# Cross attention of a decoder layer: scores as three rounded products, queries turned first, the output projection moved ahead of the first scores

## Chip, cores, metric

One Trainium2 chip, one of its cores. The metric is the device time of the whole program in microseconds (us), the median of three runs. The program holds two decoder layers; the change touches one stage of the first.

## Reference, cut to the stage

Batch 16, 112 query rows of 512 features, 375 context rows. Sixteen heads of 128, in eight groups of keys and values. The stage computes the second half of the layer's attention (`xout`), and adds its part of the projection to x:

```python
def _gqa(q, k, v):
    scale = 1.0 / np.sqrt(q.shape[-1])
    scores = jnp.einsum('bsghd,btgd->bghst', q, k) * scale
    p = jax.nn.softmax(scores, axis=-1)
    return jnp.einsum('bghst,btgd->bsghd', p, v)

qx = _fp8_linear_pertensor(ln_out, wqx, wqx_scale, qx_in_scale).reshape(b, s, g, hpg, d)
qx = _ln(qx, qxln_w, qxln_b)
kvx = jnp.einsum('bsi,oi->bso', cond, w_kv_x)
kx, vx = jnp.split(kvx, 2, axis=-1)
kx = _ln(kx.reshape(b, sc, g, d), kxln_w, kxln_b)
vx = vx.reshape(b, sc, g, d)
xout = _gqa(qx, kx, vx).reshape(b, s, nh * d)
cat = jnp.concatenate([core, xout], axis=-1)
catq = _div_clamp_fp8(cat, proj_smooth)
return jnp.einsum('bsi,oi->bso', catq, wproj) * (proj_in_scale * proj_w_scale)
```

## The kernel before

`normed_attention` (L613) is used twice, for self attention (`own` true) and for cross attention (`own` false); the change is to the second use. Its loop has 32 steps: the 16 sequences with the first eight heads, then the 16 sequences with the other eight. A step b has these parts:

- Eight `unit`s (L862), each a product of 512 columns in one PSUM bank: 0 and 1 are queries (four heads each), 2 to 4 are keys of 125 context rows each, 5 to 7 (from `LU` = 5) are values. Context and weights are held as a rounded high part and a low part (type f32r), so that a unit of keys or values is 12 matmuls (`product`, L31: high x high, low x high, high x low), a unit of queries 8.
- VectorE measures and normalises queries and keys (`measure`, `aggregate`, `normalise`, L1159 to L1181), with a root by GpSimd (L818).
- `turn` (L901): TensorE transposes eight heads of queries, then four tiles of keys (375 columns each). ScalarE evicts each with the affine part of the normalisation (`take_turned`, L1068) into `qT` and `kT`, f32.
- `scores` (L936), eight of them (heads 0 to 7), each an f32 matmul of 375 columns; VectorE takes the maxima (`top`, L1183), ScalarE the exponentials (L1081), VectorE divides (L1189 to L1201), TensorE transposes (`turn_probs`, L951), ScalarE evicts (`take_probsT`, L1091), TensorE weighs values in pairs of heads (`weigh_values`, L965).
- VectorE scales the result and prepares its rounding (L1203 to L1220), GpSimd rounds it (`round_cat`, L834), TensorE projects (`project_out`, L922: 16 matmuls of 512 columns), VectorE adds to x (`add_out`, L1244). This rounding and projection of step b - 1 lie in step b.

Query rows are padded from 112 to 128 with rows of another sequence, so that in every eighth step (b % 8 = 7, `spread`) the queries are already there, in `spread_room`, and units 0 and 1 are left out. GpSimd copies these rows (`keep_spread`, L827).

The order is written out by hand for each engine, and each engine works its queue in that order. TensorE in step b (L1008 to L1025): unit 5; last values of step b - 1; unit 6; `turn`; unit 7; scores 0 and 1; `project_out(b - 1)`; then for t from 0 to 7: scores t + 2, one of the units 0 to 4 of step b + 1 (after t = 0, 2, 3, 4, 5), `turn_probs` t, and values of a pair for t = 3, 5, 7. ScalarE (L1103): cast of the next queries' input; values 0, 1; `take_turned`; values 2; exponentials 0 and 1; `split_ctx(b + 1)` (L1060); then for each t exponential t + 2 and `take_probsT` t. VectorE (L1260, L1313): maxima 0 and 1; division 0 and 1; `split_ctx(b + 1)` (low part, L1156); `add_out(b - 1)`; from step 18 on `measure_row` (L1251); then for t = 0 the maxima of head 2, the measuring of unit 0, and so on.

`turn_probs` t waits for `probsT_ready` of the transposition before it, since all but the last share PSUM bank 5 (L957). Scores use banks 2, 3, 4 in turn (L748), turned tiles banks 6, 7, 5, 3, 2, 4 (`TBANK`, L644), the weighed values banks 6 and 7, the projection bank 6, the units banks 0 and 1.

## Time and profile before

| | |
|---|---|
| median of 3 runs | 3532.51 us (3528.98 to 3533.45) |
| profiled execution | 3518.53 us, its span 3516.8 us |
| granted TensorE clock, mean | 0.969 of full |
| cross attention | from about 855 to 2095 us of the span |
| busy over the span | TensorE 92%, VectorE 68%, ScalarE 49%, GpSimd 23% |
| one step of the cross attention (902.43 to 941.14) | 38.71 us |

How to read the rows below. PE is TensorE, DVE VectorE, ACT ScalarE, POOL GpSimd. A timeline row has start and duration in us, engine, line of the kernel, operation, what it writes and reads, its shape, how many like it in a row (x4), and in brackets how long the engine had been idle before it and for whom. A matmul's duration is its streaming and some 0.17 to 0.18 us until its end is known; the pace of several is seen in their starts. An f32 matmul makes two records (x2 for one). A row of the stretch table has the stretch, its length, then busy time (count) of PE, PEld (weight load), DVE, ACT and POOL, then the granted clock of TensorE (1.00 full, 0.50 half), the DMA share and GB/s. Matmuls through `product` all stand under L42.

### The profile page before, as it was taken

Reading aid. Unit: us, or ns where it says so; the run is one execution under the profiler, and the core shown is the slowest. Engines: PE = TensorE matmul, PEld = TensorE weight load, DVE = VectorE, ACT = ScalarE, POOL = GpSimd, SP = SyncE. Lnnn points to the kernel's source line nnn. Section 1 sums busy time; section 2 is a strip of 40 time slices with the busy share of each in tenths; the row PEclk is TensorE's granted clock in tenths of the full one; section 3 lists DMA queues with packets and bytes.
Section 4 is the critical chain, followed back from the end, with each engine's and each line's share of the span. In section 5 each row is a group of like instructions: output and inputs, shape, how many; then the busy total and the mean of one; then the engine's idle time right before and its main releaser. Section 6 shows DMA issues by size and latency. Waiting matters only on the chain. (4 is left out here: it accounts for less than half of the span.)

```text
span 3516.8 us, 50927 instructions
## 1 busy us (share of the span) xinstructions
PE 3249.5 (92%) x17776; PEld 2635.9 (75%) x17776; DVE 2386.7 (68%) x6147; ACT 1724.9 (49%) x4169; POOL 793.6 (23%) x936
## 2 busy tenths in 40 slices
PE   5858998997999999999999989999989979998999
PEld 4647877885787888778777867888868757776788
DVE  5997878786666666767667757899765555557433
ACT  5984455444344334443344333788537755452222
POOL 0004444452222222332222224000223310000000
PEclk9879999999999999999999999999999989999999
DMA  6121010002000000210000016999820124543000
GB/s 234 29 61 32 1 49 25 1 27 77 21 21 30 21 23 20 85 38 22 21 21 30 20 42 223 362 404 398 318 60 2 49 107 137 152 138 120 13 12 19
DMA packets 121167, 304.67 MB, mean 87 GB/s; under 512 B 42336, under 2 KB 45920, under 8 KB 115152
## 3 DMA queue, kind: packets, MB, share of 16 engines
q1 hardware_dynamic: 114752, 283.74, 23.0%
q0 software_dynamic: 6160, 17.67, 1.7%
q8 instruction: 144, 2.36, 0.3%
q14 instruction: 111, 0.91, 0.1%
HBM read 255.32 MB, written 45.35 MB: 85 GB/s over the span
## 5 line engine op out<-in xcount | busy, mean ns | idle before, releaser
L42 PE MATMUL bank<-w,cross_ctx_part 128*125 128x512 f32 x1536 | 519.8, 420 | 2.8 <-DVE cross_kn L1179 2.8
L42 PEld LDWEIGHTS bank<-w,cross_ctx_part 128*125 128x125 f32 x1536 | 283.4, 187 | 83.9 <-DVE cross_kn L1179 8.5
L1087 ACT ACTIVATE cross_prob<-bank,cross_neg_max 112x375 f32<-112x375 f32 x256 | 147.0, 574 | 347.5 <-DVE cross_neg_max L1185 347.5
L42 PE MATMUL bank<-w_low,cross_ctx_part 128*125 128x512 f32 x768 | 303.2, 395 | 0.0
L1185 DVE TENSOR_REDUCE cross_neg_max<-bank 112x1 f32<-112x375 f32 x256 | 134.2, 525 | 208.8 <-PE bank L947 205.7
L42 PE MATMUL bank<-moe_wt,moe_zT 128*128 128x448 f32 x1176 | 262.1, 371 | 0.6 <-DVE moe_wt L1872 0.6
L1872 DVE TENSOR_TENSOR moe_wt<-moe_raw,moe_wt 128x1792 fp32r<-128x1792 f32 (+1 forms) x111 | 231.6, 2108 | 14.5 <-ACT moe_wt L1767 13.5
L42 PE MATMUL bank<-mlp_zT,mlp_signs 128*128 128x512 f32 (+1 forms) x1024 | 221.0, 369 | 6.2 <-DVE mlp_zT L2620 6.2
L42 PEld LDWEIGHTS bank<-moe_wt,moe_zT 128*128 128x128 f32 x1176 | 213.5, 188 | 15.5 <-DVE moe_wt L1872 0.8
L42 PE MATMUL bank<-w,self_xq 128*128 128x512 f32 (+1 forms) x464 | 196.8, 424 | 22.6 <-DVE w_low L601 21.3
L1767 ACT ACTIVATE moe_wt<-moe_raw 128x1792 fp32r<-128x1792 f32 (+1 forms) x111 | 196.8, 1775 | 28.5 <-DMA moe_raw<-in_moe_w 16.8
L42 PEld LDWEIGHTS bank<-mlp_zT,mlp_signs 128*128 128x128 f32 x1024 | 177.7, 189 | 43.4 <-issue 6.4
L821 POOL TENSOR_TENSOR cross_ve<-cross_mv,eps 125x4 f32<-125x4 f32 (+1 forms) x152 | 30.3, 199 | 720.7 <-DVE cross_mv L1170 720.7
L42 PE MATMUL bank<-w_low,self_xq 128*128 128x512 f32 (+1 forms) x464 | 188.2, 406 | 0.0
L1100 ACT ACTIVATE cross_probT<-bank 125x336 f32<-125x336 f32 x256 | 111.3, 447 | 154.8 <-PE bank L961 154.7
L1179 DVE TENSOR_SCALAR cross_kn<-bank,cross_mv,cross_rstd 125x128 f32<-125x128 f32 x384 | 131.1, 404 | 80.4 <-POOL cross_rstd L824 80.2
L1066 ACT ACTIVATE cross_v<-bank 125x512 f32<-125x512 f32 x96 | 57.4, 598 | 237.8 <-PE bank L975 130.6
L947 PE MATMUL bank<-cross_kT,cross_qT 128*112 128x375 f32 x448 | 173.3, 478 | 0.0
L961 PEld LDWEIGHTS bank<-ident,cross_prob 112*125 112x125 f32 x768 | 116.5, 189 | 72.9 <-issue 40.0
L42 PEld LDWEIGHTS bank<-w_low,cross_ctx_part 128*125 128x125 f32 x768 | 143.4, 187 | 36.2
L975 PE MATMUL bank<-cross_probT,cross_v 125*128 125x224 f32 x768 | 169.9, 358 | 0.0
L42 PE MATMUL bank<-moe_wt,moe_hT 128*128 128x512 f32 x588 | 148.3, 402 | 12.2 <-issue 12.2
(436 smaller groups left out, 8131.4 us busy)
## 6 DMA issues: line engine op xcount, KB each, us to landing
moe_raw<-in_moe_w SPq DMA_DIRECT2D x74, 896.0 KB, 7.4
moe_raw<-in_moe_w SPq DMA_DIRECT2D x37, 1024.0 KB, 8.3
stream<-in_L1f SPq DMA_DIRECT2D x32, 768.0 KB, 7.7
cross_ctx_raw<-in_ctxT SPq DMA_DIRECT2D x32, 750.0 KB, 4.3
wide_ctxT<-in_ctxT SPq DMA_DIRECT2D x16, 750.0 KB, 4.2
wide_ctx_rows<-in_ctx SPq DMA_DIRECT2D x16, 750.0 KB
expert_rows<-a_zeros SPq DMA_DIRECT2D x1, 8960.0 KB, 25.7
moe_zrow<-expert_rows SPq DMA_DIRECT2D x35, 256.0 KB, 7.8
```

What stands on the lines that cost most here:

```text
L42: mm = pe.matmul(out, a, b, start=first and n == 0, stop=last and n == len(pairs) - 1)
L821: pool.tensor_tensor(ve[0:rows, n, :], mv[0:rows, n, :, 1], k.eps[0:rows, 0:4], ALU.add)\
L947: mm = pe.matmul(score_bank(t)[0:S, i * NK:(i + 1) * NK], queries[:, h, 0:S], keys[:, h // 2, 0:NK], start=True, stop=True)
L961: mm = pe.transpose(probs_bank(t)[0:KN, at:at + S], prob[:, t % SLOTS, i, j * KN:(j + 1) * KN], k.ident[0:S, 0:S])
L975: mm = pe.matmul(ps[6 + pair // 2][:, at:at + 2 * S], v[:, j, pair * P:(pair + 1) * P], probsT_of(pair, j), start=j == 0, stop=j == KT - 1)
L1066: act.activation(v[:, j, :], unit_bank(b, LU + j)[0:KN, :], ACT.Copy).then_inc(s["v_ready"], 1)
L1087: op = act.activation(prob[:, t % SLOTS, i, :], score_bank(t)[0:S, i * NK:(i + 1) * NK], ACT.Exp, bias=neg_max[:, h:h + 1], accum_out=tota ...
L1100: act.activation(probT[:, (t // 2) % 2, :, t % 2, :], probs_bank(t)[0:KN, 0:KT * S].rearrange("p (j t) -> p j t", t=S), ACT.Copy).then_inc ...
L1179: op = dve.tensor_scalar(out, unit_bank(b, n)[0:rows, h * P:(h + 1) * P], mv[0:rows, n, h, 0:1], rstd[0:rows, n, h:h + 1], ALU.subtract, A ...
L1185: dve.tensor_reduce(neg_max[:, HS * t:HS * (t + 1)], score_bank(t)[0:S, 0:HS * NK].rearrange("p (h n) -> p h n", h=HS), AX.X, ALU.max, neg ...
L1767: act.activation(wt[:, PLACES[n % 4], 0, 0:w], raw[:, n % RAW, 0:w], ACT.Copy).then_inc(s["w_high"], 1)
L1872: dve.tensor_tensor(wt[:, PLACES[n % 4], 1, 0:w], raw[:, n % RAW, 0:w], wt[:, PLACES[n % 4], 0, 0:w].bitcast(F32), ALU.subtract).then_inc( ...
```

## The change

- Scores of the cross attention become three f32r products of 376 columns (`product` of `qT_high`, `qT_low`, `kT_high`, `kT_low`); the 376th column is a zero pad, set once. ScalarE evicts each turned tile twice, raw and rounded (`split_turned`). GpSimd subtracts to make the low parts (`queries_low`, `keys_low`; in a spread step `spread_queries_low`), which lie where the raw ones lay.
- `turn` is split: the queries are turned first in a step, ahead of unit 5, the keys where they were. In step 0 the queries wait for the last normalisation. ScalarE evicts the queries first in its step, ahead of the cast. Turned tiles use banks 2, 3, 5, 6, 4, 7.
- `project_out(b - 1)` goes ahead of scores 0 and 1 where there is a next step with query units (`out_first`); it also waits for the eviction of key tile 1. Where there is none, it stays behind them.
- GpSimd's `round_cat(g - 1)` stands in step g behind the low parts of the queries and ahead of those of the keys; before it stood at the end of step g - 1's queue.
- The bf16 tiles `clipped` and `magic` now lie in `probT`.

```diff
-    TBANK = [2, 3, 4] if own else [6, 7, 5, 3, 2, 4]
+    TBANK = [2, 3, 4] if own else [2, 3, 5, 6, 4, 7]
...
+            qT_high, kT_high = sb("qT", [P, H, P], F32R), sb("kT", [P, GR, NK + 1], F32R)
+            qT, qT_low = raw_and_low(k, ctx, "cross_qT", [P, H, P])
+            kT, kT_low = raw_and_low(k, ctx, "cross_kT", [P, GR, NK + 1])
...
+            def turned_by(g, n):
+                pool.wait_ge(s["turned_raw"], turned_no(g, n))
+                pool.wait_ge(s["turned_ready"], turned_no(g, n))
+
+            def queries_low(g, n):
+                turned_by(g, n)
+                heads = slice(4 * n, 4 * n + 4)
+                pool.tensor_copy(spread_qT[:, heads, spread_rows(g)], qT[:, heads, S:]).then_inc(s["spread_ready"], 1)
+                pool.wait_ge(s["spread_ready"], 2 * tiles(g) + n + 1)
+                pool.tensor_tensor(qT_low[:, heads, :], qT[:, heads, :], qT_high[:, heads, :].bitcast(F32), ALU.subtract)\
+                    .then_inc(s["turned_low"], 1)
...
+            def keys_low(g, n):
+                turned_by(g, n)
+                pool.tensor_tensor(kT_low[:, n - 2, 0:NK], kT[:, n - 2, 0:NK], kT_high[:, n - 2, 0:NK].bitcast(F32), ALU.subtract)\
+                    .then_inc(s["turned_low"], 1)
...
-                if not spread(g):
+                if own and not spread(g):
                     keep_spread(g)
+                if not own:
+                    if spread(g):
+                        spread_queries_low(g)
+                    for n in range(0 if spread(g) else 2):
+                        queries_low(g, n)
+                    if g:
+                        round_cat(g - 1)
+                    for n in range(2, TG):
+                        keys_low(g, n)
...
-            def turn(b):
-
-                if not own:
-                    wait(pe, s["cat_scaled"], 2 * b)
+            def turn_queries(b):
                 for g in range(0 if spread(b) else 2):
-                    pe.wait_ge(s["normed"], norm_no(b, g))
+                    pe.wait_ge(s["normed"], norm_no(b, LU - 1 if not own and b == 0 else g))
...
+            def turn_keys(b):
+
+                if not own:
+                    wait(pe, s["cat_scaled"], 2 * b)
...
+                if not own and not at_end:
+                    pe.wait_ge(s["turned_raw"], turned_no(b + 1, 3))
+                    pe.wait_ge(s["turned_ready"], turned_no(b + 1, 3))
...
+                    if t == 0 and spread(b):
+                        pe.wait_ge(s["spread_low"], b // GROUP + 1)
+                    if t in (0, 2, 6):
+                        pe.wait_ge(s["turned_low"], turned_no(b, (2, 4, 4, 5)[t // 2]))
+                    if t >= 3:
+                        pe.wait_ge(s["exp_done"], NS * b + t - 2)
+                    mm = product(pe, score_bank(t)[0:S, 0:NK + 1], [q[:, t, 0:S] for q in (qT_high, qT_low)],
+                                 [key[:, t // 2, :] for key in (kT_high, kT_low)], True, True)
...
+                    turn_queries(b)
                     unit(b, LU)
                     if not first:
                         weigh_values(b - 1, GR - 1)
                     unit(b, LU + 1)
-                    turn(b)
+                    turn_keys(b)
                     unit(b, LU + 2)
+                    out_first = not first and one_more and has(b + 1, 0)
+                    if out_first:
+                        project_out(b - 1)
                     scores(b, 0)
                     scores(b, 1)
-                    if not first:
+                    if not first and not out_first:
                         project_out(b - 1)
...
+            def split_turned(b, n):
+                act.wait_ge(s["turned_in_psum"], turned_no(b, n))
+                for first, to in ((qT, kT), (qT_high, kT_high)):
+                    out = to if n >= 2 else first
...
+                    op = act.activation(out, ps[TBANK[n]][:, 0:out.shape[1]], ACT.Identity, scale=head_ln[:, at:at + 1],
+                                        bias=head_ln[:, at + 1:at + 2])
...
+                if not own:
+                    split_queries(b)
                 if one_more:
                     cast(b + 1)
...
                     take_values(b, 0)
                     take_values(b, 1)
-                take_turned(b)
+                    for n in range(2, TG):
+                        split_turned(b, n)
                 take_values(b, KT - 1)
```

## Rows read from the trace of the kernel before

**Rows 1.** The page, busy time and share of the span.

```profile
PE 3249.5 (92%) x17776; PEld 2635.9 (75%) x17776; DVE 2386.7 (68%) x6147; ACT 1724.9 (49%) x4169; POOL 793.6 (23%) x936
```

**Rows 2.** The table of stretches, one step of the cross attention (step 1 to 2).

```profile
902.43:941.14 38.71, 38.71 (x190) 31.11 (x188) 25.77 (x96) 15.77 (x35) 10.06 (x13) 1.00 0.08 24
```

**Rows 3.** The timeline of step 12, TensorE.

```profile
1313.33 0.78 PE L42 MATMUL bank<-w,cross_ctx_part 128*125 128x512 f32 x2
...
1316.26 1.30 PE L975 MATMUL bank<-cross_probT,cross_v 125*128 125x224 f32 x6
...
1320.18 1.03 PE L908 MATMUL bank<-ident,cross_qn 128*128 128x128 f32 x8
...
1325.12 1.42 PE L947 MATMUL bank<-cross_kT,cross_qT 128*112 128x375 f32 x4
...
1326.61 0.40 PE L42 MATMUL bank<-wo_low,cross_catq 128*112 128x512 f32 x1
...
1329.84 0.39 PE L42 MATMUL bank<-wo_low,cross_catq 128*112 128x512 f32 x1
...
1333.67 0.55 PE L961 MATMUL bank<-ident,cross_prob 112*125 112x112 f32 x3
```

**Rows 4.** The timeline of step 12, ScalarE, GpSimd and VectorE.

```profile
1320.88 1.45 ACT L1078 ACTIVATE cross_qT<-bank,head_ln 128x512 f32<-128x512 f32 x2
...
1321.79 1.90 POOL L838 TENSOR_TENSOR cross_catq<-cross_scaled,cross_magic 128x896 fp32r<-128x896 f32 x1
1322.22 2.32 ACT L1078 ACTIVATE cross_kT<-bank,head_ln 128x375 f32<-128x375 f32 x4
...
1327.73 1.45 ACT L1060 ACTIVATE cross_ctx_part<-cross_ctx_raw 128x1500 fp32r<-128x1500 f32 x1
...
1329.21 1.72 DVE L1156 TENSOR_TENSOR cross_ctx_part<-cross_ctx_raw,cross_ctx_part 128x1500 fp32r<-128x1500 f32 x1 [0.73 <-ACT cross_ctx_part L1060]
...
1331.45 0.54 DVE L1185 TENSOR_REDUCE cross_neg_max<-bank 112x1 f32<-112x375 f32 x1
...
1333.07 0.45 ACT L1100 ACTIVATE cross_probT<-bank 125x336 f32<-125x336 f32 x1 [0.39 <-PE bank L961]
```

**Rows 5.** Timelines elsewhere: f32r products of 256 and of 448 columns.

```profile
3466.83 3.13 PE L42 MATMUL bank<-mlp_zT,mlp_signs 128*128 128x256 f32 x25
...
2149.64 0.97 PE L42 MATMUL bank<-moe_wt,moe_zT 128*128 128x448 f32 x4
```

**Rows 6.** GpSimd's low parts by line; the timeline of step 19.

```profile
L594 POOL TENSOR_TENSOR w_low<-w_raw,w x8: 1272/1308/2277, 1439.5 to 1465.8; 128x512 fp32r<-128x512 f32 x8
...
1617.06 0.69 DVE L1254 BATCH_NORM_STATS2 cross_row_stats<-x 112x6 f32<-112x512 f32 x1
...
1619.38 0.55 PE L961 MATMUL bank<-ident,cross_prob 112*125 112x112 f32 x3
```

**Rows 7.** The timeline of step 0, which has no output projection.

```profile
840.74 2.83 DVE L1179 TENSOR_SCALAR cross_kn<-bank,cross_mv,cross_rstd 125x128 f32<-125x128 f32 x8
...
854.37 2.06 PE L947 MATMUL bank<-cross_kT,cross_qT 128*112 128x375 f32 x6
...
860.09 0.54 DVE L1185 TENSOR_REDUCE cross_neg_max<-bank 112x1 f32<-112x375 f32 x1
...
861.81 0.55 PE L961 MATMUL bank<-ident,cross_prob 112*125 112x112 f32 x3 [2.59 <-ACT cross_probT L1100]
```

**Rows 8.** TensorE's idle times (timeline), and the clock behind them (table of stretches).

```profile
842.21 0.71 PE L42 MATMUL bank<-w,cross_ctx_part 128*125 128x512 f32 x2 [2.79 <-DVE cross_kn L1179]
...
1450.64 0.55 PE L961 MATMUL bank<-ident,cross_prob 112*125 112x112 f32 x3 [3.70 <-ACT cross_probT L1100]
...
843.60:847.00 3.40, 3.40 (x10) 2.61 (x9) 0.00 (x0) 0.45 (x1) 0.00 (x0) 0.50 0.00 0
861.80:865.20 3.40, 3.39 (x17) 2.77 (x18) 2.84 (x11) 1.01 (x3) 1.21 (x2) 1.00 0.48 194
...
1451.20:1454.60 3.40, 3.40 (x8) 2.34 (x8) 2.74 (x9) 1.54 (x5) 0.89 (x1) 0.50 0.94 355
```

61 lines of the change are left out of this document (42 added, 19 removed).

## Prediction

> **What bounds the kernel now.** I read the page's busy shares first: TensorE is busy 92% of the span [rows 1]. Then the stretch table of one step of the cross attention, because only that stage (855 to 2095 us, 32 steps) is changed: in a step of 38.71 us TensorE is busy for all of it, VectorE 25.8, ScalarE 15.8, GpSimd 10.1 [rows 2]. So the stage looks bound by TensorE's work, and cheaper scores look like pure gain. The timelines show why that is not enough. In step 12 [rows 3] TensorE starts the last value units at 1313.33, the first scores at 1325.12 (11.79 later; I call the start of scores 0 S), and transposes the second head's probabilities at 1333.67, S + 8.55. Beside it [rows 4], the other engines are busy with one strict chain from S on, since ScalarE and VectorE work their queues in written order: maxima and exponentials of heads 0 and 1, ScalarE's high part of the next context (1327.73, 1.45), VectorE's low part (1329.21, 1.72), the addition of the output rows, the maxima of head 2 (1331.45, S + 6.33), its exponential, and only then `take_probsT` of head 0 (1333.07), for which the second transposition waits. During these 8.55 us TensorE does four scores, the output projection, query unit 0 and one transposition. The chain and TensorE's work end nearly together there: ScalarE had idled only 0.39 us for TensorE. The output projection is what covers the chain.
>
> **Cost of a score.** The projection's second product starts at 1326.61, its sixteenth at 1329.84 [rows 3]: 3.23/14 = 0.231 for each f32r product of 512 columns, 3.70 for the sixteen. The first of them would so start at 1326.38, and the two scores ahead, from 1325.12, take 1.26, 0.63 each. The new ones are three f32r products of 376 columns. The trace has f32r products of 256 and 448 columns [rows 5]: 25 in 3.13 us, less 0.28 for a single one, is 0.119 each; 4 in 0.97, less 0.37, is 0.200. Between them on a line 376 columns give 0.17, so a score 0.51 and a gain of 0.12. Bounds of one product: 0.119 and 0.231 (512 columns), a score 0.36 to 0.69. If all 256 gains counted: 31 us. The Trainium skill (FP8 and Floating Point Precision, TensorE Precision Notes) says true f32 goes through the array in four passes; the trace agrees (0.63 us for 375 columns), and three passes for four would by that rule alone be 0.47 a score, and the sum below 4 us less.
>
> **Queries turned first, and its cost at the top of a step.** The same eight transpositions (1320.18, 1.03 less 0.17 until the end is known: 0.87 us) [rows 3], only earlier; nothing for TensorE. ScalarE now evicts each turned tile twice, raw and rounded: two more of 128x512 and four more of 128x375. Back to back they take 1.45/2 = 0.73 and 2.32/4 = 0.58 [rows 4], so 3.8 us more of ScalarE a step, out of 23 idle. Whether that blocks anything I follow from the top T of step (1313.33 before). TensorE: turned queries to T + 0.87, value unit to 3.7, last values of the step before to 4.8, value unit to 7.6, keys turned to 8.9, value unit to 11.8; then the projection. ScalarE: queries from 0.6 to 3.6, cast, values at 5.0 and 7.8, then keys at 0.58 each: key tile 1 (the one that holds the projection's bank 6) is out at about 10.8, the last at 13.1. Cover 1.0 us. GpSimd: two query tiles (0.29 + 1.31 each, [rows 6] for 128x512) done at 5.5; then `round_cat`, which before ended at 1321.79 + 1.90 = 1323.69, that is 6.3 after the last values end (1316.26 + 1.13) [rows 3, 4], so now T + 11.2. TensorE asks for it at 11.8: cover 0.6. Then four key tiles; 128x375 costs between 0.8 (in proportion to 896 columns at 1.90) and 1.31, I take 1.1: done at 12.3, 13.4, 14.5, 15.6. Scores 0 come at T + 15.5 behind the projection, scores 2, which want three tiles, at 16.5. So all this is hidden; if the cover is gone it costs what runs over, 1:1. VectorE's queue is not changed.
>
> **The projection ahead of the scores.** `out_first` holds for steps 1 to 29 without 6, 14 and 22: 26 steps. S moves from T + 11.79 to 11.79 + 3.70 = T + 15.49. Everything in the chain above hangs on S or is queued behind something that does: the exponentials on scores 0 and 1, `split_ctx` of the next step behind them on ScalarE, its low part, `add_out` and the maxima of head 2 behind it on VectorE. So the chain moves 3.70 later with S, while the 3.70 of TensorE work that covered it now lies before it. Step 0 has no projection, and shows this directly [rows 7]: S = 854.37, the maxima of head 2 at S + 5.72, the second transposition at 861.81 = S + 7.44 after 2.59 us of idle TensorE. It has no `add_out` either; steps 1 to 17 have it, and their maxima of head 2 come 6.33 - 5.72 = 0.61 later. Less 0.12 for the faster first score, the second transposition comes at S + 7.44 + 0.61 - 0.12 = S + 7.93. TensorE gets there at four scores 2.04 + unit 1.85 + transposition 0.32 = S + 4.2. It stands still for 3.7 us. From step 18 on `measure_row` (0.69 us, [rows 6]) is also ahead of the maxima, some 0.6 more: S + 8.53, a stall of 4.3. Before, that row reading was hidden but for 0.1: in step 19 (S = 1610.74) the second transposition came at 1619.38, S + 8.64 [rows 6].
> Sum of a step, up to 17: S + 3.70, chain 7.93 - 8.55 = -0.62, four later scores at -0.12 = -0.48, together +2.60. From 18 on: 3.70 - 0.12 - 0.48 = +3.10. Behind the stall nothing catches up, since TensorE had no other idle time in the step. Steps 1 to 17 that count: 14 (15 apart), +36.4; 18 to 29: 11, +34.1. Step 15: its maxima wait for VectorE's weight splitting, there TensorE idled 3.70 already [rows 8], so the projection moves into time that was lost anyway: 0. Step 0: queries now turned ahead of the first value unit, behind VectorE's last key normalisation, which ends at 840.74 + 2.83 = 843.57 where TensorE resumed at 842.21 [rows 7, 8]: +1.4, less 0.1. Steps 6, 14, 22, 30 and 31 keep the scores first; scores 0 wait for GpSimd's first key tile (12.3 for 11.8, +0.6) and the later scores give 0.5 back; GpSimd's last key tiles run beside VectorE: +0.5 each, +2.5. Sum without the clock: 36.4 + 34.1 + 1.3 + 2.5 = **+74**.
>
> **The clock.** TensorE's granted clock fell from full (2.4 GHz) to half (1.2) after it had idled 2.79 us (842.21) and after 3.70 us (1450.64), and stayed at half for about 3.4 us of work each time; after the 2.59 us in step 0 it stayed full [rows 8]. A half-speed stretch of 3.4 us costs 1.7. The new stalls, 3.7 and 4.3 us, are as long as the longer of these or longer, in 25 steps, in each of which TensorE is the bound afterwards. Bounds: 0 (as after 2.59) and 3.4 (two such stretches running); I take 1.7, by the 3.70 row: 25 x 1.7 = **+43**. The Trainium skill (TensorE: Matmul & The Clock Gate, Part 1) has the rule that activity releases the throttle and idleness brings it back; the trace agrees, and without that rule the sum would be +74.
>
> Total 74 + 43 = +117. The profiled execution, 3518.5 us (span 3516.8), would become about 3636. It lies 14 us under the median of the timed runs, so I add the sum to the median: 3532.5 + 117 = **3650**.
>
> **The rivals.** (A) The stall comes, the clock doesn't fall or falls rarely: for it, the case of 2.59; against it, two falls at 2.79 and 3.70. 3532.5 + 74 = 3607. Chance 0.2. (B) The other side: TensorE stays the bound, because the next context's split and the maxima of head 2 get done early enough, as they would if they didn't hang on S; then 256 scores at -0.12 give -31: 3502. The point from which it decides: the second transposition must be ready by S + 4.2; step 0, without the projection, had it at 7.44. Chance 0.07. (C) GpSimd overruns: `round_cat` has 0.6 of cover at the projection; if the low parts take as long as 128x896 (1.90), the queries end at about 6.6 and let it start in time (11.2 less its two 1.9 is 7.4), but a key tile at 1.9 makes scores 2 wait for T + 16.9, 0.4 later: 25 x 0.45 = 11, 3661. Beside it: the Trainium skill (SBUF — State Buffer, SBUF: two separate sides) states that GpSimd and a VectorE operation with two SBUF inputs lock each other out of one port pair; by that rule a low part that meets `cat_clipped` would be held for its 0.6 us, the same size; the trace agrees that a low part can be held, 2.28 for a median of 1.31 [rows 6]. Chance 0.05. (D) The f32r products go at the pace of 512 columns: a score 0.69, the four later ones +0.24 for -0.48, 25 x 0.72 = 18: 3668. Chance 0.04. (E) The cut: if part of the stall is absorbed so that it just pays for the scores, no change. Nothing in the rows absorbs it. Chance 0.02.
>
> **How the numbers follow.** Forecast 3650, chance 0.62. A measurement of this kernel can tell about 0.2%, 7 us, from no change. Faster: B, 0.07. Same: E, 0.02. Slower: forecast, A, C and D, 0.91. The range goes from below A, 3595, to the forecast with two half-speed stretches in about half of the steps together with C or D, 3690 (1.7 x 13 + 18 = 40 more).
>
> **What would show it.** TensorE's wait for `take_probsT` at L961 should be about 100 us in all, once a step, some 3.6 long up to step 17 and 4.2 from 18; S-to-S about 41.3 to 43 for 38.71; scores 0.51 each; the maxima of head 2 at S + 6.2; no wait at `project_out`; half clock after most of the stalls. Wrong would be: maxima of head 2 much before S + 6, a wait ahead of the projection, a period of 37.7.

## The result, and the profile after

| | before | after |
|---|---|---|
| median | 3532.98 us (4 runs) | 3661.74 us (4 runs, 3657.19 to 3670.66) |
| ratio | 1 | 1.0367 (1.0354 to 1.038) |
| profiled execution, its span | 3518.53, 3516.8 | 3670.66, 3668.9 |
| granted TensorE clock, mean | 0.969 | 0.944 |

Slower by 129 us, 3.7%; the forecast was 3650, in 3595 to 3690. The page of after, busy time, answers to [rows 1]: TensorE's share falls although it has 256 more matmul records, GpSimd's work grows by a quarter.

```profile
PE 3294.8 (90%) x18032; PEld 2731.6 (74%) x18032; DVE 2390.0 (65%) x6147; ACT 1838.9 (50%) x4357; POOL 1002.3 (27%) x1154
```

The table of stretches of after (columns as in [rows 2]): one step up to 17 and one from 18 on, from scores 0 to scores 0, against 38.71 in [rows 2]; then a stretch right behind the stall of the first, and the one behind that.

```profile
950.94:993.75 42.81, 39.36 (x198) 33.59 (x197) 25.89 (x96) 19.28 (x41) 16.84 (x20) 0.96 0.07 21
1734.53:1778.89 44.36, 40.32 (x197) 34.46 (x196) 26.53 (x98) 19.29 (x41) 16.80 (x20) 0.92 0.06 18
...
959.92:963.30 3.38, 3.38 (x11) 2.69 (x10) 2.50 (x8) 1.09 (x4) 0.34 (x1) 0.51 0.02 9
963.36:966.70 3.34, 3.34 (x17) 2.82 (x17) 2.82 (x15) 1.12 (x3) 1.22 (x2) 1.00 0.00 0
```

The timeline of after, step 2 (counted from 0, as in [rows 3]), TensorE: queries turned (the top T), the projection's first product, scores 0 and 1, the second transposition of probabilities. It answers to [rows 3].

```profile
935.58 1.04 PE L942 MATMUL bank<-ident,cross_qn 128*128 128x128 f32 x8
...
947.25 0.39 PE L42 MATMUL bank<-wo,cross_catq 128*112 128x512 f32 x1
...
950.94 0.33 PE L42 MATMUL bank<-cross_kT,cross_qT 128*112 128x376 f32 x1
951.11 0.33 PE L42 MATMUL bank<-cross_kT,cross_qT_low 128*112 128x376 f32 x1
951.28 0.33 PE L42 MATMUL bank<-cross_kT_low,cross_qT 128*112 128x376 f32 x1
951.45 0.34 PE L42 MATMUL bank<-cross_kT,cross_qT 128*112 128x376 f32 x1
...
958.79 0.55 PE L1016 MATMUL bank<-ident,cross_prob 112*125 112x112 f32 x3 [3.45 <-ACT cross_probT L1177]
```

The same step, VectorE, then ScalarE, the chain that this transposition waits for. It answers to [rows 4].

```profile
954.84 1.72 DVE L1238 TENSOR_TENSOR cross_ctx_part<-cross_ctx_raw,cross_ctx_part 128x1500 fp32r<-128x1500 f32 x1 [0.72 <-ACT cross_ctx_part L1120]
956.47 0.68 DVE L1330 TENSOR_TENSOR x<-bank,x 112x512 f32<-112x512 f32 x1
957.07 0.54 DVE L1267 TENSOR_REDUCE cross_neg_max<-bank 112x1 f32<-112x375 f32 x1
...
957.65 0.57 ACT L1164 ACTIVATE cross_prob<-bank,cross_neg_max 112x375 f32<-112x375 f32 x1 [2.84 <-DVE cross_neg_max L1267]
...
958.21 0.44 ACT L1177 ACTIVATE cross_probT<-bank 125x336 f32<-125x336 f32 x1
```

The waits of TensorE in the stage (total, times, longest), after:

```profile
PE bank L1016 <- ACT cross_probT L1177: 112.3, 36, 4.0
PE bank L1016 <- DVE cross_prob L1282: 15.0, 4, 6.8
...
PE bank L42 <- POOL cross_catq L842: 4.2, 1, 4.2
PE bank L42 <- POOL cross_kT_low L863: 1.5, 5, 0.4
```

What is to be seen: the projection starts at 947.25 with no wait, scores 0 follow it at 950.94 = T + 15.36. A product of 376 columns takes 0.17 (950.94, 951.11, 951.28), a score 0.51. From S = 950.94 the maxima of head 2 come at S + 6.13 and the second transposition at S + 7.85, after 3.45 us in which TensorE did nothing. The low part of the next context at 954.84, the addition at 956.47 and the maxima at 957.07 stand behind each other on VectorE: that is the chain. Before, the same wait for `take_probsT` was 18.0 us in 11 places, at most 3.7.

### The profile page after: what moved, and what is told of

It reads as the page before. It is cut to its first block and busy times, and to the rows that moved or that the text cites. A ratio compares the mean times of both kernels' runs of the same rounds, so it can differ in the third digit from the quotient of the medians.

```text
span 3668.9 us, 52101 instructions
## 1 busy us (share of the span) xinstructions
PE 3294.8 (90%) x18032; PEld 2731.6 (74%) x18032; DVE 2390.0 (65%) x6147; ACT 1838.9 (50%) x4357; POOL 1002.3 (27%) x1154
## 5 line engine op out<-in xcount | busy, mean ns | idle before, releaser
L42 PE MATMUL bank<-w,cross_ctx_part 128*125 128x512 f32 x1536 | 495.8, 404 | 0.0
L1016 PE MATMUL bank<-ident,cross_prob 112*125 112x112 f32 x768 | 134.3, 293 | 127.9 <-ACT cross_probT L1177 112.3
L1016 PEld LDWEIGHTS bank<-ident,cross_prob 112*125 112x125 f32 x768 | 129.2, 209 | 157.2 <-issue 123.1
L1953 DVE TENSOR_TENSOR moe_wt<-moe_raw,moe_wt 128x1792 fp32r<-128x1792 f32 (+1 forms) x111 | 231.7, 2109 | 14.7 <-ACT moe_wt L1848 14.3
L1245 DVE BATCH_NORM_STATS2 cross_stats<-bank 125x6 f32<-125x128 f32 (+1 forms) x608 | 134.6, 285 | 46.1 <-PE bank L42 46.1
L42 PE MATMUL bank<-moe_wt,moe_hT 128*128 128x512 f32 x588 | 152.4, 410 | 11.1 <-issue 11.1
```

The lines of the kernel that those rows point to most:

```text
L42: mm = pe.matmul(out, a, b, start=first and n == 0, stop=last and n == len(pairs) - 1)
L1016: mm = pe.transpose(probs_bank(t)[0:KN, at:at + S], prob[:, t % SLOTS, i, j * KN:(j + 1) * KN], k.ident[0:S, 0:S])
L1245: dve.bn_stats(stats[0:rows, n, h, :], unit_bank(b, n)[0:rows, h * P:(h + 1) * P]).then_inc(s["stat"], 1)
L1953: dve.tensor_tensor(wt[:, PLACES[n % 4], 1, 0:w], raw[:, n % RAW, 0:w], wt[:, PLACES[n % 4], 0, 0:w].bitcast(F32), ALU.subtract).then_inc( ...
```

## The experiments

The steps are compared by the time from one second transposition of probabilities to the next ("a step" below; it has the number of the step in which it ends, so that step 3 of after is the one that begins at 958.79). In the kernel before it is 38.71 us (steps 2 to 5) and 38.76 (from 18 on), in after 41.4 to 44.4, by how often the clock fell in it (in e3, up to step 17, 41.9 and 43.4 in turn). The experiments ran on four chips. On that of e1 to e4 the kernel before stands at 3530.5, on the others at 3518.6 to 3520.0, so ratios are what to compare.

| kernel | ratio to before | step 3 | step 26 |
|---|---|---|---|
| after | 1.0367 (1.0354 to 1.038) | 42.81 | 44.35 |
| e1, projection behind | 1.004 (1.0026 to 1.0054) | 38.97 | 38.98 |
| e2, stall filled | 1.0257 (1.0239 to 1.0274) | 41.4 | 42.05 |
| e3, before, projection ahead | 1.0343 (1.0319 to 1.0368) | 41.86 | 44.07 |
| e4, split early | 1.0122 (1.0105 to 1.0139) | 39.30 | 41.30 |
| e5, e1 and key low part sooner | 1.0014 (1.0004 to 1.0023) | 38.41 | 38.59 |
| e6, e5 and split early | 1.0152 (1.0135 to 1.0169) | 39.73 | 40.38 |
| e7, e4 and chain short | 1.0087 (1.007 to 1.0104) | 39.28 | 40.07 |
| e8, e5 and VectorE's gaps | 0.9982 (0.9973 to 0.9991) | 38.45 | 38.47 |
| e9, before and VectorE's gaps | 0.9987 (0.9978 to 0.9996) | 38.71 | 38.76 |
| e10, e7 and VectorE's gaps | 1.0011 (1.0002 to 1.002) | 38.66 | 38.71 |
| e11, e8 and halved measurement | 1.0127 (1.011 to 1.0144) | 40.20 | 40.55 |
| e12, e9 and halved measurement | 1.015 (1.0133 to 1.0167) | 40.70 | 40.89 |

### Is it the place of the projection?

```diff
# e1_out_behind, against after
-                    out_first = not first and one_more and has(b + 1, 0)
+                    out_first = False
# e3_before_out_first, against before
+                    out_first = not first and one_more and has(b + 1, 0)
+                    if out_first:
+                        pe.wait_ge(s["turned_ready"], turned_no(b, TG - 1))
+                        project_out(b - 1)
                     scores(b, 0)
                     scores(b, 1)
-                    if not first:
+                    if not first and not out_first:
                         project_out(b - 1)
```

> The changed kernel with the output projection put back behind scores 0 and 1 in every step; products, evictions and GpSimd's low parts stay. Theory (the moved projection uncovers the chain context split, maxima of head 2, take_probsT 0): the stall of 3.45 and 4.05 us goes, half clock goes; left are 8 x 0.12 gained a step, less 0.3 to 0.5 for scores 0 waiting for GpSimd's first key tile and, from step 18, 0.5 for the chain: 3510 to 3525 us. Rival 1 (the doubled evictions and the low parts cost the time): it stays near 3650. Rival 2 (half and half): near 3590.

> The kernel before with one edit, the projection ahead of scores 0 and 1 in the same 26 steps; f32 scores, one eviction, queries turned where they were. Theory: the projection alone makes the loss. TensorE reaches the second transposition at S + 4.7, the chain at S + 8.05 (8.65 from step 18): a step longer by 3.2 and 3.7, 85 us in all, and the clock 30 to 60 more: 3650 to 3680. Rival (the double evictions and low parts make it): 3533 to 3545.

e1 came out at 3545.27 (ratio 1.004, 15 us over the median of before), e3 at 3648.82 (1.0343, 118 over). So the moved projection alone makes nearly all of the loss, and taking it out of the change gives nearly all of it back. In e3 the second transposition comes at S + 8.04 with 3.18 us of idle (8.64 and 3.77 from step 18 on), as expected. One of its rows (timeline, TensorE):

```profile
1083.24 0.55 PE L961 MATMUL bank<-ident,cross_prob 112*125 112x112 f32 x3 [3.17 <-ACT cross_probT L1104]
```

But e1 missed: 3510 to 3525 was expected, since the cheaper scores should have been a gain of 18 us. It is a loss of 14. One step of e1 and its row of waits, against 38.71 in [rows 2]:

```profile
982.52:1021.48 38.96, 38.43 (x196) 32.20 (x197) 25.96 (x96) 19.25 (x42) 16.64 (x21) 1.00 0.08 24
...
PE bank L42 <- POOL cross_kT_low L863: 14.7, 31, 6.2
...
1408.08 0.43 PE L42 MATMUL bank<-cross_kT,cross_qT 128*112 128x376 f32 x1 [0.27 <-POOL cross_kT_low L863]
```

TensorE works 38.43 and waits the rest. In every step scores 0 wait for GpSimd's low part of key tile 0, some 0.3 us, and in step 15 6.2. Why they do is followed up in e5.

### What does the clock cost?

```diff
# e2_stall_filled, against after: 19 (from step 18 on 22) products into a free bank
+                        if t == 1 and out_first:
+                            pe.wait_ge(s["turned_low"], turned_no(b, 5))
+                            for i in range(19 if b < B + 2 else 22):
+                                pe.matmul(ps[7][0:S, 0:NK + 1], qT_high[:, 0, 0:S], kT_high[:, 0, :], start=True, stop=True)
                         turn_probs(b, t)
```

> The changed kernel with 19 (from step 18 on 22) needless products of 376 columns in each of the 26 steps, put where TensorE stands still, ahead of the second transposition; their result is not used. They take 3.25 and 3.76 us of stalls of 3.6 and 4.2. Theory (a part of the loss is the granted clock, which halves after each stall): full clock through the stage, period of a step 41.4 up to step 17 and 41.8 after, time 3532.5 + 74 = about 3607, in spite of some 530 more products. Rival (the clock is no part of it, the records only show it): 3661 or more, by the products that run over.

3621.70, ratio 1.0257, 15 us over the 3607 expected. The products' output is used by nothing; they only keep TensorE busy in the stall. The steps are as expected up to 17 (41.4) and 0.25 longer from 18 on; the rest of the miss is in steps 0, 1, 15 and 16. Step 26 from one second transposition to the next, with the granted clock at 1.00, where after had 0.92 in such a step:

```profile
1924.46:1966.50 42.04, 41.76 (x218) 36.09 (x219) 26.23 (x100) 19.13 (x41) 16.65 (x20) 1.00 0.07 22
```

After's 3.67% less these 2.57% is 1.1% of 3530 us, 39 us: the price of the clock (46 in the stage of the two profiled executions, 1399.1 and 1352.9 us). The remaining 91 us are the stall itself and what steps 0, 1, 15 and 16 add. The two parts are not cleanly apart: e2 leaves the waits of those four steps unfilled or filled in part, and over the stage the granted clock is 0.94 in after, 0.98 in e2 and 0.99 before. So a few of the 91 us are still the clock's. A filled stall is as long as an idle one, so what waits there is not TensorE's work.

### Is it the chain that hangs on the scores?

```diff
# e4_split_early, against after (ScalarE; the same in VectorE's step ahead of top(b, 0))
+                early = not own and b and one_more and has(b + 1, 0)
+                if early:
+                    split_ctx(b + 1)
                 exponential(b, 0)
                 exponential(b, 1)
...
-                    else:
+                    elif not early:
                         split_ctx(b + 1)
```

> The changed kernel with the split of the next context ahead of exponential 0 on ScalarE and ahead of the maxima of head 0 on VectorE, in the 26 steps with the projection ahead. Theory (what the projection covered is this split, 1.45 + 1.72 us, behind the first exponentials): it now runs under the projection; the second transposition comes at about S + 6.2, the stall falls to about 2.0 (2.6 from step 18), too short for half clock in most steps: 3560 to 3585. Rival (the split is not in the chain, the maxima wait for the scores alone): no change, 3661.

3574.38, ratio 1.0122, within what was expected: two thirds of the loss is gone by moving one item of ScalarE's queue and one of VectorE's. Timelines of e4, VectorE and TensorE, step 3 (S = 987.28):

```profile
986.63 1.80 DVE L1241 TENSOR_TENSOR cross_ctx_part<-cross_ctx_raw,cross_ctx_part 128x1500 fp32r<-128x1500 f32 x1 [7.56 <-ACT cross_ctx_part L1120]
...
993.03 0.55 PE L1016 MATMUL bank<-ident,cross_prob 112*125 112x112 f32 x3 [1.34 <-ACT cross_probT L1177]
```

The split now lies beside the projection: VectorE had idled 7.56 us ahead of it. The second transposition comes at S + 5.75 and not S + 7.85. At 1.34 us of idle the clock stays full; from step 18 on (1.93) many steps again show a half-speed stretch (39.95 us without, 41.30 with one).

### Where did the scores' gain go, and does a short chain free the projection?

```diff
# e5_key_low_sooner, against e1 (GpSimd's step)
-                    if g:
-                        round_cat(g - 1)
-                    for n in range(2, TG):
+                    if g:
+                        pool.wait_ge(s["cat_magic"], g)
+                        pool.tensor_tensor(scaled[:], clipped, magic[:], ALU.add).then_inc(s["cat_shifted"], 1)
+                    keys_low(g, 2)
+                    if g:
+                        pool.wait_ge(s["cat_shifted"], g)
+                        pool.tensor_tensor(catq[:], scaled[:], magic[:], ALU.subtract).then_inc(s["cat_rounded"], 1)
+                    for n in range(3, TG):
                         keys_low(g, n)
# e6_behind_early: e5 with the edit of e4
# e7_first_short, against e4: ScalarE, then VectorE
                 for t in range(NS):
+                    if early and t == 0:
+                        take_probsT(b, t)
                     if t + AHEAD < NS:
                         exponential(b, t + AHEAD)
-                    take_probsT(b, t)
+                    if not early or t:
+                        take_probsT(b, t)
...
-                    if not first:
+                    if not first and not early:
                         add_out(b - 1)
-                    if b >= B + 2:
+                    if b >= B + 2 and not early:
                         measure_row(b - B - 2)
...
                         if t + AHEAD < NS:
                             top(b, t + AHEAD)
+                        if early and t == 0:
+                            add_out(b - 1)
+                            if b >= B + 2:
+                                measure_row(b - B - 2)
```

> The kernel after with the projection behind scores 0 and 1 in every step, as in e1_out_behind, and GpSimd's low part of key tile 0 put between the two operations of round_cat instead of behind both. In e1 scores 0 waited for that low part in 31 steps, 14.7 us in all: it was done at T + 12.05 (T the start of the turned queries), because the second operation of round_cat (9.20 to 11.11) stood ahead of it, though the tile was evicted at T + 9.51. Theory: that queue place is what eats most of the scores' gain in e1. The low part is then done at T + 10.6, before the unit ahead of scores 0 ends, the second operation of round_cat ends at T + 12.6, about when the projection asks for it (T + 12.7). Expected: the wait of scores 0 for GpSimd's key low part gone (below 2 us), period 38.97 -> about 38.5, time 3545 - 14 = 3531, 3525 to 3538. Rival: the rest of the step is bound by VectorE's queue (the maxima, normalisations and measurements), which had the wait as slack; then the 0.4 us come back as waits further down the step, and the time stays at 3540 to 3546.

> e5_key_low_sooner with the next context's split (ScalarE's high part, VectorE's low part) ahead of the exponential and the maxima of head 0 in steps 1 to 30 without 6, 14, 22 and 30. With the projection behind scores 1 the second transposition of probabilities comes at S + 8.2 in any case, so there is room for the split (1.45 + 1.72) ahead of the maxima of head 0, and VectorE is free for the maxima of head 2 as soon as score 2 is there, at S + 5.3 instead of S + 6.2. Theory: in e1 the last part of the step (second to eighth transposition, 17.06 us, where the kernel after had 16.69) waited for VectorE, which was late by that 0.9; with VectorE sooner that part comes down to 16.7 and the period to 38.1 or less, time 3505 to 3522: the rounded scores then pay, in the old order of the projection. Rival: VectorE is bound by its sum, or the maxima of head 0 now hold up the first transposition; then nothing below e5.

> The kernel after, with its projection ahead of the scores, and with all of the chain that stood between the scores and the second transposition taken out of the way: the split ahead of the maxima and the exponential of head 0 as in e4_split_early, ScalarE's take of head 0's transposed probabilities ahead of the exponential of head 2, VectorE's output addition and row statistics behind the maxima of head 2. In e4 (3574) the second transposition stood 1.34 to 1.93 us. Theory: its wait is for nothing but these queued parts. First transposition at S + 3.42, its eviction ends 0.8 later, second at S + 4.6, TensorE there at S + 4.4: 0.2 us of idle, full clock in every step up to 30. Period 38.71 - 0.96 + 0.2 = about 38.0; stage minus 18 against before, with steps 0, 15 and 16 (+5 and +6) as they were in e4: 3532 - 18 + 11 = 3525, range 3510 to 3545. Rival: head 2's chain, later by the same order, gives the stall to the third transposition; then 3550 to 3575.

e5: ratio 1.0014, 0.26% or 9 us below e1, of the 14 expected. The low part of key tile 0 is done at 1019.12, a microsecond ahead of scores 0 (1020.15); GpSimd's queue, e5:

```profile
1015.71 1.89 POOL L878 TENSOR_TENSOR cross_scaled<-cross_probT 128x896 f32<-128x896 bf16 x1 [1.81 <-DVE cross_probT L1306]
1018.13 0.99 POOL L863 TENSOR_TENSOR cross_kT_low<-cross_kT_raw,cross_kT 128x375 fp32r<-128x375 f32 x1 [0.53 <-ACT cross_kT L1151]
1019.08 1.90 POOL L882 TENSOR_TENSOR cross_catq<-cross_scaled,cross_probT 128x896 fp32r<-128x896 f32 x1
```

The wait for the key low part falls from 14.7 us in 31 places to 3.4 in one (step 15); a step is 38.41. Its queue place behind `round_cat` was the cause. The rounded scores pay 0.3 us a step now, of the 0.96 that eight should give. All of it lies ahead of the second transposition (S + 8.23 for S + 8.54); the part from there to the eighth, with the last four scores, is 17.05 as in the kernel before.

e6: the wrong way, 1.0152. The split fits ahead of the maxima only when the projection lies there too. With the projection behind, nothing is between unit 7 and scores 0, so VectorE gets the high part late, and its low part is in front of the maxima (e6, step 3, S = 984.90):

```profile
987.93 2.26 DVE L1246 TENSOR_TENSOR cross_ctx_part<-cross_ctx_raw,cross_ctx_part 128x1500 fp32r<-128x1500 f32 x1 [7.56 <-ACT cross_ctx_part L1125]
990.11 0.99 DVE L1275 TENSOR_REDUCE cross_neg_max<-bank 112x1 f32<-112x375 f32 x2
```

Maxima of head 0 at S + 5.2, 0.7 in e5; second transposition at S + 9.9 with 1.64 of idle. My expectation counted room for the split there and did not ask when ScalarE has the high part: it starts at S + 1.5 (986.39), behind ScalarE's eviction of the last values.

e7: ratio 1.0087, where 3525 against 3532, 0.998, was expected. The stall is gone: the second transposition comes at S + 4.53 with 0.12 of idle, the clock is full behind it. But the part from there to the eighth transposition takes 17.9 us (18.7 from step 18 on) where after needs 16.69 at full clock. VectorE, then TensorE, e7 step 3 (second transposition at 991.32):

```profile
990.66 0.68 DVE L1336 TENSOR_TENSOR x<-bank,x 112x512 f32<-112x512 f32 x1
991.26 0.88 DVE L1251 BATCH_NORM_STATS2 cross_stats<-bank 128x6 f32<-128x128 f32 x4
...
994.09 1.37 DVE L1267 TENSOR_SCALAR cross_qn<-bank,cross_mv,cross_rstd 128x128 f32<-128x128 f32 x4 [0.53 <-POOL cross_rstd L829]
...
995.60 0.71 PE L42 MATMUL bank<-w,cross_ctx_part 128*125 128x512 f32 x2 [0.31 <-DVE cross_qn L1267]
```

The stall has moved to the units: unit 2 waits for the bank that VectorE's normalisation of unit 0 frees. The rival that was named for e7, a stall ahead of the third transposition, has about this time (1.0087 of 3532 is 3563) but is not what happened: the trace has no idle time there.

### VectorE's queue

```diff
# e8_vector_gaps, against e5; e9_before_gaps: the same against before; e10_first_gaps: against e7,
# where the addition and the row statistics are taken from both of their places
-                    if not first:
-                        add_out(b - 1)
-                    if b >= B + 2:
-                        measure_row(b - B - 2)
...
-                        if b >= B + 2 and t == 0:
+                        if b >= B + 2 and t == 4:
                             aggregate_row(b - B - 2)
                         if 1 <= t and t + 2 < NS:
                             invert(b, t + 1)
                             probabilities(b, t + 1)
+                        if not first and t == 1:
+                            add_out(b - 1)
+                        if b >= B + 2 and t == 3:
+                            measure_row(b - B - 2)
```

> e5_key_low_sooner (projection behind the scores, key low part sooner) with VectorE's output addition taken from ahead of the maxima of head 2 to the place behind the division of head 2 (there VectorE waits about 0.45 us in each of five rounds for GpSimd's root of the next unit), and its row statistics likewise two rounds later. In e5 the part from the second to the eighth transposition is 17.05 us, as in the kernel before, while after, whose VectorE had slack from the stall, has 16.69: VectorE works there without a pause except those 0.45, at 4.03 us a unit. Theory: VectorE's queue is what keeps the rounded scores from paying there. With 0.5 to 0.6 us taken off ahead of it and put into the pauses, the part is 16.7, the idle of 0.59 ahead of the second transposition in steps 18 to 29 falls to 0.12, the period is 38.05, the time 0.35 x 14 + 0.55 x 12 = 11 us below e5: ratio to before 0.9983, between 0.997 and 0.9995. Rival: TensorE waits for something else there (the score's own eviction chain), then ratio as e5, 1.0014.

> The kernel before with the same change of VectorE's queue and nothing else. Theory: before, TensorE's own work fills the step and VectorE is only just in time beside it, so a faster VectorE brings nothing but the 0.10 us ahead of the second transposition in steps 18 to 29 and some of the 1.35 in the spread steps: ratio 0.998 to 1.000. If it gives more than 0.2%, VectorE's queue was already the bound before and what e8 gains is no gain of the rounded scores.

> e7_first_short (projection ahead of the scores, the chain behind the scores shortened) with the same change of VectorE's queue. In e7 the second transposition came at S + 4.53 with 0.12 of idle, but the part behind it took 17.9 us (18.7 from step 18 on) for 16.69: VectorE starts it later against TensorE, because the projection no longer lies between. Theory: the place of the projection costs nothing by itself; it decides how much time VectorE has between the scores and the second transposition. Taking 0.6 (and from step 18 0.6 more) off VectorE there gives 17.3, period 38.65 in every step, time about 0.6 x 13 + 1.3 x 12 = 23 us below e7: ratio to before 1.002, 1.000 to 1.005. Rival: the part behind is set by ScalarE or the transpositions: ratio as e7, 1.0087.

e10: 1.0011, as expected; a step of 38.66 and 38.71, the part behind the second transposition 17.3. So with the projection ahead of the scores, and the split, the take, the addition and the row statistics put elsewhere, the loss of 3.7% is down to 0.1%. It is not quite nothing: with the projection behind them and the same VectorE queue, e8 stands at 0.9982 and e9, the kernel before, at 0.9987, so 0.3% (10 us) is left between e10 and e8, 0.22 us of it in each step (38.66 for 38.44). One step of it:

```profile
985.00:1023.65 38.65, 38.39 (x197) 32.23 (x196) 25.42 (x97) 19.13 (x41) 16.65 (x20) 1.00 0.08 25
```

e8: 0.9982, the forecast number, by another way: the steps up to 17 did not change (38.45; the part stays at 17.07), the gain is around the four spread steps (steps 6 and 7: 37.72 and 35.53 for 38.30 and 36.86) and from 18 on (38.47 for 38.60), where the row statistics had stood in the way. e9: 0.9987, so before gains nearly as much from the same edit, also ahead of spread steps (37.69 for 38.21). The difference of e8 and e9 lies within both intervals. The rounded scores are worth 0.27 us a step there, but steps 0, 1 and 15 are 1.5, 1.3 and 3.8 longer. In the whole e8 is 2.5 us below e9 by the medians and 3.1 by the profiled stage, and that it is a gain is not shown.

```diff
# e11_halved_measure, against e8; e12_before_halved: the same against e9
# (`measure` now takes the heads that it measures)
+                        halved = one_more and t in NEXT_AT and t - 1 in NEXT_AT and has(b + 1, NEXT_AT[t - 1])
+                        if halved:
+                            measure(b + 1, NEXT_AT[t], range(2))
                         if one_more and t - 1 in NEXT_AT and has(b + 1, NEXT_AT[t - 1]):
                             normalise(b + 1, NEXT_AT[t - 1])
...
-                                measure(b + 1, NEXT_AT[t])
+                                measure(b + 1, NEXT_AT[t], range(2 if halved else 0, 4))
```

> e8_vector_gaps with VectorE's measurement of a unit in two halves: the statistics of two heads ahead of the normalisation of the unit before, the other two behind it. In e8 the part from the second to the eighth transposition stayed at 17.07, although VectorE's maxima of head 2 were 0.6 sooner: the last unit starts 12.39 behind the second transposition in before, e1, e5 and e8 alike. Theory: VectorE works there in rounds of 4.03 us, one for each unit (normalisation 1.37, measurement 0.88, aggregation 0.5, maxima 0.5, division 0.5, and 0.45 of waiting for GpSimd's root), that begin with the end of unit 0 and not with anything ahead of it, and a unit needs the bank that the normalisation two before it frees; TensorE's round with the cheaper score would be shorter. With 0.44 us of the measurement in the wait, a round of VectorE takes 3.6 and TensorE's own sets the pace: the last unit starts 12.05 behind the second transposition, the part takes 16.7, the period 38.08, the time 0.36 x 27 = 10 us below e8: ratio to before 0.9955, between 0.9945 and 0.9965. Rival: ScalarE's exponentials or the evictions set the round, then ratio as e8, 0.998.

> e9_before_gaps with the same halves, that is the kernel before with both changes of VectorE's queue. Theory: with the f32 score TensorE's own round is 4.03 as well (in before its score ends when the bank comes free), so a faster VectorE brings nothing: ratio as e9, 0.998 to 0.9995. The difference of e11 to this one is what the rounded scores are worth once nothing else holds the step: about 0.6 us a step, 18 us with those at scores 0 and 1, less 6 for steps 0, 15 and 16. Rival: before was held by VectorE too and gains as much as e11.

Both missed, by 1.7% and 1.5%: 1.0127 and 1.015, slower. What I had taken for a pause to be filled put a wait for TensorE ahead of what TensorE waits for. First the kernel before, VectorE and TensorE; then e8; then e11, each around the last unit of a step:

```profile
1344.63 1.37 DVE L1179 TENSOR_SCALAR cross_kn<-bank,cross_mv,cross_rstd 125x128 f32<-125x128 f32 x4 [0.44 <-POOL cross_rstd L824]
1345.48 0.80 PE L947 MATMUL bank<-cross_kT,cross_qT 128*112 128x375 f32 x2
1346.05 0.73 PE L42 MATMUL bank<-w,cross_ctx_part 128*125 128x512 f32 x2
```

```profile
1304.13 1.37 DVE L1266 TENSOR_SCALAR cross_kn<-bank,cross_mv,cross_rstd 125x128 f32<-125x128 f32 x4 [0.44 <-POOL cross_rstd L829]
...
1305.07 0.34 PE L42 MATMUL bank<-cross_kT_low,cross_qT 128*112 128x376 f32 x1
1305.55 0.73 PE L42 MATMUL bank<-w,cross_ctx_part 128*125 128x512 f32 x2
```

```profile
1283.55 0.50 DVE L1250 BATCH_NORM_STATS2 cross_stats<-bank 125x6 f32<-125x128 f32 x2 [1.32 <-PE bank L42]
1283.97 1.35 DVE L1266 TENSOR_SCALAR cross_kn<-bank,cross_mv,cross_rstd 125x128 f32<-125x128 f32 x4
...
1285.37 0.73 PE L42 MATMUL bank<-w,cross_ctx_part 128*125 128x512 f32 x2 [1.02 <-DVE cross_kn L1266]
```

In e11 the half measurement waits 1.32 us for the end of a unit, the normalisation behind it starts at 1283.97, and the next unit starts at 1285.37, 0.05 behind its end (1285.32); it comes 13.30 us behind the second transposition where it came 12.39 in e8. In e8 too it starts 0.05 behind the end of that normalisation (1305.50), though the score ahead of it is done. In before both meet. The normalisation ends at 1346.00 and the unit starts at 1346.05, again 0.05 behind it; but its third product comes at 1346.62, 1.13 behind the start of the score ahead of it, and in units 2 and 3 of that step it comes 1.10 behind (their first product starts 0.35 behind the score, the last unit's 0.57). So VectorE held TensorE up by only 0.03 us. It is shown, then, that VectorE's normalisation releases the last unit in e8 and e11, and that before TensorE's work and VectorE's queue arrived together, within 0.05 us. A gain of TensorE alone could not come out there. That a shorter VectorE round would let the scores pay was argued, and e11 could not show it: it lengthened the queue's wait instead. It stays open. Against each other e11 and e12 show the rounded scores 0.5 us a step ahead up to step 17 (40.20 for 40.70) and 0.3 behind it, of which 0.3 is again ahead of the second transposition; the intervals of the two ratios overlap a little.

## Why the prediction was right

**The bound, and the chain.** Right. The chain behind S was to bring the maxima of head 2 to S + 6.2 and the second transposition to S + 7.93; after shows 6.13 and 7.85. From step 18 on S + 8.53 was forecast, 8.45 came. The wait for `take_probsT` was to be about 100 us; it is 112.3, with 36 entries because step 0, step 15 and the steps that keep the scores first have theirs too. e3 and e1 show the cause, e4 the chain, e10 that little else stood in the way (1.0011).

**The score.** Right in the size, 0.51 a score by 0.17 a product, read off a line between 256 and 448 columns [rows 5]. The Trainium skill (FP8 and Floating Point Precision, TensorE Precision Notes) by its four passes for one gave 0.47; the rows decide, 0.51. That the four later scores of a step gain came out in part, 0.36 us for the 0.48, and only because of the stall: behind it VectorE had time in hand, and the part up to the eighth transposition took 16.69 at full clock against 17.05. That was luck of a kind. Rival B, TensorE stays the bound and 256 scores pay 31 us, would have failed even with the chain out of the way, since e5 and e10 show a gain of 0.3 and 0.05 a step and not 0.96. The prediction read 38.71 of 38.71 busy for TensorE as "bound by TensorE's work" and did not ask how far behind VectorE was: 0.05 us.

**The sum without the clock.** Forecast +74, measured by e2 +91. A step up to 17 is 41.37 to 41.40 in e2, +2.68 for the forecast 2.60, and 42.05 from 18 on, +3.29 for 3.10. By the terms: the projection ahead is 3.73 for 3.70, the chain -0.69 for -0.62, the later scores -0.36 for -0.48. The 25 steps make 74 where the sum had 70.5. Most of the rest is in two places where a term failed:

- *Step 15: 0* was wrong, the largest error of a term. The projection was to move into time lost anyway. It did not start: it waited 4.22 us for `round_cat`. And the stall of the other steps, 3.25 us here, came on top. Timelines of after, VectorE, GpSimd, TensorE:

```profile
1488.43 9.98 DVE L601 SCALAR_TENSOR_TENSOR w_low<-w_raw,raw_scale,w 128x1024 fp32r<-128x1024 f32 x4
...
1488.93 2.77 POOL L858 TENSOR_TENSOR cross_qT_low<-cross_spread_room,cross_qT 128x896 fp32r<-128x896 f32 x1 [6.08 <-ACT cross_qT L1153]
1491.66 2.86 POOL L840 TENSOR_TENSOR cross_scaled<-cross_probT 128x896 f32<-128x896 bf16 x1
1494.60 2.74 POOL L842 TENSOR_TENSOR cross_catq<-cross_scaled,cross_probT 128x896 fp32r<-128x896 f32 x1
...
1497.39 0.77 PE L42 MATMUL bank<-wo,cross_catq 128*112 128x512 f32 x1 [4.22 <-POOL cross_catq L842]
```

  `round_cat` now stands behind a low part of the queries, and beside VectorE's weight splitting each GpSimd operation of 896 columns takes 2.74 to 2.86 us where `round_cat`'s take 1.88 to 1.91 in every other step. VectorE's four splits take 1.28, 3.15, 2.90 and 2.89, the first begun before GpSimd's. The cover of 0.6 us that I had worked out for an ordinary step was used for one that is none. Steps 15 and 16 together grew by 8.65 us (45.98 and 44.22 for 40.06 and 41.49), by 11.3 in e2, where the sum had 0 and 2.6 and the clock. In e2 the clock fell once more there, behind the stall of 1.59 us in step 14, which cost 1.5. The Trainium skill (SBUF — State Buffer, SBUF: two separate sides) has the rule that a VectorE operation with two SBUF inputs and GpSimd lock each other out; the rows agree with it, since the ends alternate between the engines (VectorE 1489.71, GpSimd 1491.70, VectorE 1492.78, GpSimd 1494.52, and so on): VectorE's come 1.1 us behind GpSimd's, GpSimd's 1.7 to 2.0 behind VectorE's. I had weighed the rule at 0.6 us in an ordinary step, beside `cat_clipped`, which reads one SBUF tensor and not two, and which no low part of the queries meets in the trace; I had not weighed it in the step where VectorE does nothing else for 10 us.

- *Steps 0 and 1* were +1.3 and +2.6, and +6.2 came (32.42 and 53.84 for 30.92 and 49.16). The late queries cost 1.5, near the 1.3. What the sum left out is that the stall of step 0, 2.59 us before, became 2.79, as TensorE arrives sooner by the cheaper scores, and that the clock now fell behind it (0.50 from 864.4 to 867.8). e1, where the projection is not moved, shows the same two steps 1.5 and 1.9 longer.

**The clock.** +43 forecast, 39 measured by the medians, 46 by the profiled stage (both a little short, since e2 keeps some falls of its own), but as a sum of parts that differ: none to two half-speed stretches a step. Behind the stalls of 3.45 us in steps 1 to 13 the part up to the eighth transposition is 1.2 to 1.45 above its 16.69 in eight steps, 2.7 in three, nothing in one; behind those of 4.04 us it is 2.25 to 2.4 in all eleven. The 1.7 that I took from a single row lies between; that it comes near the mean of these 23, some 1.9, is luck. The Trainium skill (TensorE: Matmul & The Clock Gate, Part 1) says that idleness brings the throttle back; the trace agrees, and e2, which takes away the idleness and leaves the wait, shows it here.

**The covers.** Right: GpSimd's `round_cat` ended at T + 11.1 (11.2 forecast), the projection started at T + 11.67 without a wait in all steps but 15; key tile 1 was out at T + 10.6 (10.8); the low parts of the keys were done by T + 14.9 (15.6), as 128x375 takes 1.00 us and not 1.1. Only where the scores come first does the key low part matter, 1.5 us in five steps here, 14.7 in e1. In the cases without the projection ahead the forecast had +0.6 for it.

**What is left.** The stage of the profiled execution (first product of a key unit to last product of the last projection) grew from 1264.5 to 1399.1, by 134.6 us, 17.6 more than the sum of 117: 3.2 in the 25 steps, 8.7 in steps 15 and 16 (of e2), 2.3 in steps 0 and 1, 3.2 of clock. The 8.7 and the 2.3 have falls of the clock in them, so that its share is rather more and theirs less. Behind the stage the profiled execution of after took 17 us longer than before's (1438.6 and 1421.4, in the expert layer). In e1 to e12, whose code there is the same, this part took 1426 to 1432 in the four runs on the chip where before has a median of 3530.5, and 1420 to 1425 in the eight on the others. The profiled execution of before, 3518.53, lies at the level of those others and 14 us under its timed runs, so the 17 us go, in the main, with the chip and not with the change, as far as these runs tell. The medians differ by 129 us and the two profiled executions by 152: before's lies 14 under its median and after's 9 above.

## What to carry to other kernels

Work that lies between two dependent points of a chain is cover for that chain; before it is moved ahead of the chain's start, list by queue everything that hangs on that start, and move first what does not need it (here one split on ScalarE and one on VectorE, worth two thirds of a 3.7% loss). That an engine is busy for all of a step does not say by how much: subtract, at each place where it takes a buffer, when the other engine had released it, since savings beyond that slack are lost. And when a pause is filled with a part of the next item, ask first whether that item is there already: in a strict queue an early half can wait, and everything behind it with it.

## What the runs showed of the hardware

- The clock's level behind a short idle is no clear function of its length: with 1.34 us in each step it stayed full in all twelve such steps of e4 up to 13, with 1.64 it fell to half in two of twelve in e6, with 1.93 from step 18 on behind some and not behind others (e4, steps of 39.95 and 41.30 us), with 3.18 in seven of twelve, nearly in turn (e3), with 3.45 in eleven of twelve, once or twice (after). A stretch of 3.4 us at 959.92 had 0.51, the level of 1.2 GHz, and the one right behind it 1.00.
- GpSimd's two-input operation of 128x375 in f32 took 1.00 us in after (1.97 the one that began beside VectorE's last split of step 15), of 128x896 1.90, and 2.74 to 2.86 beside VectorE's two-input operation of 128x1024, which itself took 2.9 to 3.2 there and 1.28 where it began first.
- An f32r product of 376 columns started 0.17 us behind the one before; of 512 columns 0.23.
